# A decoder layer in fp32 on one core: the value products of five cross attention units in one pass over four shared PSUM banks, and weight turns alternating with query projections

## The reference, cut to what matters

```
q = (queries @ Wq + bq).reshape(b_s, nq, H, D_K).transpose(0, 2, 1, 3)
k = (keys @ Wk + bk).reshape(b_s, nk, H, D_K).transpose(0, 2, 1, 3)
v = (values @ Wv + bv).reshape(b_s, nk, H, D_V).transpose(0, 2, 1, 3)
att = jnp.einsum('bhqd,bhkd->bhqk', q, k) / jnp.sqrt(jnp.float32(D_K))
att = att * attention_weights
att = jnp.where(attention_mask, -jnp.inf, att)
att = jax.nn.softmax(att, axis=-1)
out = jnp.einsum('bhqk,bhkd->bhqd', att, v)
out = out.transpose(0, 2, 1, 3).reshape(b_s, nq, H * D_V)
return out @ Wo + bo
```

## Time and profile before

| | |
|---|---|
| median of 3 runs | 582.8 us (581.6 to 583.47) |
| the profiled execution | 583.38 us, span 581.5 us, mean granted TensorE clock 0.995 |
| PE busy | 562.7 us, 97% of the span |
| DVE busy | 441.7 us, 76% |
| ACT busy | 326.0 us, 56% |
| POOL busy | 232.7 us, 40% |
| stages 2 to 6 (161.12 to 337.88 us) | 176.76 us, of which PE is busy 175.99 |

### The profile page before, as it was taken

The page is one execution under the profiler, slowest core; times in us unless marked ns, Lnnn a source line. Parts: engine busy times, 40 slices in busy tenths (PEclk is TensorE's granted clock), DMA queues, the critical chain, the costliest instruction groups (busy, mean ns, idle before and its releaser), DMA issues.

```text
span 581.5 us, 11126 instructions
## 1 busy us (share of the span) xinstructions
PE 562.7 (97%) x3656; PEld 426.0 (73%) x3656; DVE 441.7 (76%) x838; ACT 326.0 (56%) x1005; POOL 232.7 (40%) x228
## 2 busy tenths in 40 slices
PE   8999999999999999999999999999999999999992
PEld 6547566788697978888788787878777776676661
DVE  3999999999886879958788679866677556566651
ACT  3632424368869796795976939715232245555220
POOL 1010110307590834477334581626235433444434
PEclk9999999999999999999999999999999999999997
DMA  8920004162741231522316107892654443343424
GB/s 302 349 100 2 1 1 174 45 217 91 275 152 68 93 127 34 185 74 90 130 37 218 55 23 231 261 393 94 172 129 83 64 67 62 54 67 48 60 31 45
DMA packets 36183, 68.37 MB, mean 118 GB/s; under 512 B 5504, under 2 KB 29024, under 8 KB 33632
## 3 DMA queue, kind: packets, MB, share of 16 engines
q1 hardware_dynamic: 28208, 57.99, 29.9%
q0 software_dynamic: 6784, 8.95, 9.3%
q10 hardware_dynamic: 1136, 0.73, 0.4%
HBM read 56.62 MB, written 15.25 MB: 124 GB/s over the span
## 4 chain that ended last, share of the span: by engine, by line
PE 56%; DVE 20%; DMA 9%; issue 8%; POOL 4%; ACT 2%; POOLq 0%; DVEq 0%; SPq 0%
PE pb L744 7%; DMA out_dram<-R 6%; PE pb L636 6%; DVE R L1140 6%; PE pb L499 6%; PE pb L601 6%; PE pb L549 6%; PE pb L565 5%; PE pb L516 4%; PE pb L648 4%; PE pb L778 4%; DVE R L1163 3%; PE pb L613 2%; PE pb L569 2%; DMA out_dram<-R,hidx 2%
## 5 line engine op out<-in xcount | busy, mean ns | idle before, releaser
L896 ACT ACTIVATE R<-R,mx 128x154 f32<-128x154 f32 x256 | 104.4, 415 | 0.1
L1761 POOL DMA_INDIRECT out_dram<-R x36 | 56.1, 1557 | 82.9 <-DMA out_dram<-R 41.7
L744 PE MATMUL pb<-R 128*128 x256 | 81.0, 459 | 0.0
L1022 ACT ACTIVATE R<-R 128x352 f32<-128x352 f32 x36 | 17.9, 497 | 90.4 <-DVE R L1572 74.9
L744 PEld LDWEIGHTS pb<-R 128*128 128x128 f32 x256 | 46.2, 190 | 20.4
L499 PE MATMUL pb<-xnT,wq 128*128 128x256 f32 x256 | 58.2, 383 | 0.0
L887 ACT ACTIVATE R<-pb,bq 128x256 f32<-128x256 f32 x64 | 30.1, 474 | 47.9 <-PE pb L499 47.8
L499 PEld LDWEIGHTS pb<-xnT,wq 128*128 128x128 f32 x256 | 47.7, 190 | 7.8 <-issue 1.2
L908 ACT COPY R<-pb 128x512 f32<-128x512 f32 x80 | 40.8, 614 | 18.4 <-PE pb L549 18.3
L1685 POOL DMA_INDIRECT xs_dram<-xn,pos x32 | 31.7, 991 | 47.3 <-DVE pos L1324 39.0
L896 ACT ACTIVATION_READ_ACCUMULATOR R<-R,mx 128x1 f32 x256 | 49.5, 193 | 0.0
(11 more groups left out here) (202 smaller groups left out, 1179.1 us busy)
## 6 DMA issues: line engine op xcount, KB each, us to landing
R<-in_fside_dram SPq DMA_DIRECT2D x16, 1232.0 KB, 5.6
R<-in_L_ffn_w_dram SPq DMA_DIRECT2D x16, 352.0 KB
R<-in_mask_dram SPq DMA_DIRECT2D x16, 308.0 KB, 2.9
R<-xs_dram SPq DMA_DIRECT2D x32, 129.0 KB, 2.1
KV<-in_ebias_dram SPq DMA_DIRECT2D x2, 1440.0 KB
out_dram<-x SPq DMA_DIRECT2D x4, 512.0 KB
R<-in_L_ffn_w_dram SPq DMA_DIRECT2D x8, 256.0 KB, 4.3
x<-in_x_dram SPq DMA_DIRECT2D x3, 512.0 KB, 10.9
```

The source lines that it names most:

```text
L744: ins = e.matmul(pb[:, u.i, 0:F], xsT[:, s % 2, k, :], ew13[:, bass.ds(w_reg[s] * 1408 + q * 704 + k * F, F)], start=(k == 0), stop=(k == 1))
L896: ins = e.activation(att[t % 3][:, h, :], att[t % 3][:, h, :], ACT.Exp, bias=mx[:, a4, 1, h:h + 1], accum_out=mx[:, a4, 2, h:h + 1])
L1761: e.indirect_dma_start(out=out, out_offset=bass.IndirectOffsetOnAxis(ap=to.bitcast(U32), axis=0), in_=rows, in_offset=None, compute_op=ALU ...
```

## The change

It touches units 1 to 5 (`WHOLE`), that is, stages 2 to 6.

1. **One product a unit.** `product_whole` takes four banks once. Half 0 of the heads goes to columns 0 to 255, half 1 to columns 256 to 511. All 16 matmuls of 128 rows come first, then all 16 of 32 rows. DVE drains it with two additions of 2 banks x 512 columns each instead of four of 2 banks x 256.
2. **Turns and queries alternate.** PE does 4 queries, then 2 banks of turned weights and 1 query in turn, four times, then the last 2 banks. ACT copies in the same order.
3. **What stood between moves.** `place` goes ahead of the product, `turned(*BETWEEN[n])` behind it. On ACT `normalise` and `turned` come one after the other behind the last of the ten weight copies. On DVE the product comes behind the last `top`.
4. `combined` reads `oT` in the order 0, 1, 4, 5, 2, 3, 6, 7, so that its first four steps need only the first addition.

The core of the diff:

```
+            def product_whole(u8):
+                b = u8 // 4
+                uses = [u for g in range(2) for u in bank.take_pair(("av", u8, g))]
...
+                for hf in range(2):
+                    cols = slice(256 * hf, 256 * hf + 256)
+                    for n in range(8):
+                        u, to = uses[n // 2], 64 * (n % 2 ^ n // 4)
+                        w.wait_ge(free[u.e], u.empty)
+                        e.matmul(pb[to:to + 64, u.i, cols], vm[b][:, 8 * hf + n, :], turned_in(hf, n),
+                                 start=(hf == 0), stop=False)
+                for hf in range(2):
+                    cols = slice(256 * hf, 256 * hf + 256)
+                    for g in range(2):
+                        for r in (0, 2, 1, 3):
+                            u, to = uses[2 * g + r // 2], 64 * (r % 2 ^ g)
+                            ins = e.matmul(pb[to:to + 64, u.i, cols], vr[b][32 * r:32 * r + 32, 2 * hf + g, :],
+                                           turned_in(hf, 8 + g)[32 * r:32 * r + 32, :], start=False, stop=(hf == 1))
+                            if hf and r % 2:
+                                ins.then_inc(full[u.i], 1)
+            def turned_amid_queries(u8):
...
+                queries(u8 + 2, range(0, 4))
+                for n in range(5):
+                    for hf, k in divmod(2 * n, 5), divmod(2 * n + 1, 5):
+                        weights_turned(u8, hf, k)
+                    if n < 4:
+                        queries(u8 + 2, range(4 + n, 5 + n))
-                    for j in range(8):
-                        d = bank["av", u8, j // 4, j // 2 % 2, 0]
+                    for j in (0, 1, 4, 5, 2, 3, 6, 7):
+                        d = bank["av", u8, j // 2 % 2, 0] if u8 in WHOLE else bank["av", u8, j // 4, j // 2 % 2, 0]
                 elif u8 < 7:
-                    queries(u8 + 1)
+                    turned_amid_queries(u8 - 1)
+                    if u8 in (4, 6):
+                        place(u8 // 2 - 2)
+                    product_whole(u8 - 1)
+                    if u8 in BETWEEN:
+                        turned(*BETWEEN[u8])
```

On ACT:

```
+                elif u8 < 7:
+                    queries(u8 + 1, range(0, 4))
+                    for n in range(5):
+                        for hf, k in divmod(2 * n, 5), divmod(2 * n + 1, 5):
+                            evacuate(u8 - 1, hf, k, k + 1)
+                        if n < 4:
+                            queries(u8 + 1, range(4 + n, 5 + n))
+                    if u8 in BETWEEN:
+                        normalise(*BETWEEN[u8])
+                        turned(*BETWEEN[u8])
+                    else:
+                        exps(t0, range(0, 2))
```

On DVE:

```
+            def product_whole(u8):
...
+                for g in range(2):
+                    u, v = bank["av", u8, g, 0], bank["av", u8, g, 1]
...
+                    e.tensor_tensor(
+                        oT[:, :, :].rearrange("p (f b) q -> p f b q", f=2)[:, :, 2 * g:2 * g + 2, :],
...
+                            [P, 2, 2, 256]), ALU.add).then_inc(free[u.i], 1)
-                if u8 < 7:
-                    product(u8 - 1, 0)
+                if u8 == 1:
+                    product(0, 0)
                 if u8 in (4, 6):
                     place(u8 // 2 - 2)
                 if u8 < 7:
                     top(t1, (0, H))
-                product(u8 - 1, 1)
+                if u8 - 1 in WHOLE:
+                    product_whole(u8 - 1)
+                else:
+                    product(u8 - 1, 1)
```

More of the change, by code:

```diff
@@ L138 @@
 PHI = [("k", 0), ("k", 1), ("q", 0), ("q", 1)]
+WHOLE = range(1, 6)
 SPLIT = [(1, 0), (3, 3)]
@@ L572, in product, with turned_in @@
                             ins.then_inc(full[u.i], 1)
+            def product_whole(u8):
+                b = u8 // 4
+                uses = [u for g in range(2) for u in bank.take_pair(("av", u8, g))]
+                def turned_in(hf, n):
+                    d = bank["pT", u8, hf, n // 2]
+                    w.wait_ge(free[d.i], d.drained)
+                    return pT[:, hf, n, :]
+                for hf in range(2):
[15 more added lines that the diff above has]
+            def turned_amid_queries(u8):
+                for n in range(3):
+                    d = bank["con", B - 1, n]
+                    w.wait_ge(free[d.i], d.drained)
+                queries(u8 + 2, range(0, 4))
[4 more added lines that the diff above has]
+                        queries(u8 + 2, range(4 + n, 5 + n))
             def values(u8, between, amid=None, turning=None):
@@ L691, in _ @@
                     queries(2, range(7))
+                    values(0, None, None, lambda: queries(2, range(7, 8)))
                 elif u8 < 7:
-                    queries(u8 + 1)
+                    turned_amid_queries(u8 - 1)
[4 more added lines that the diff above has]
+                        turned(*BETWEEN[u8])
                 else:
                     shared_out(*FILL[6])
-                values(u8 - 1, BETWEEN.get(u8), (lambda: place(u8 // 2 - 2)) if u8 in (4, 6) else None,
-                       (lambda: queries(2, range(7, 8))) if u8 == 1 else None)
+                    values(6, BETWEEN[7])
                 if u8 - 1 in FILL and u8 < 7:
@@ L902, in evacuate @@
                 for i in range(4 if u8 else 0):
-                    d = bank["av", u8 - 1, hf, i // 2, i % 2]
+                    d = bank["av", u8 - 1, i // 2, i % 2] if u8 - 1 in WHOLE else bank["av", u8 - 1, hf, i // 2, i % 2]
                     w.wait_ge(full[d.i], d.filled)
@@ L972, in _ @@
                 gating = u8 >= 3 and u8 % 2
-                if u8 < 7:
-                    queries(u8 + 1, range(7 if u8 == 1 else 8))
-                evacuate(u8 - 1, 0, 0, 5)
                 if u8 == 1:
+                    queries(2, range(7))
+                    evacuate(0, 0, 0, 5)
                     queries(2, range(7, 8))
[L978 to L981, removed]
+                    evacuate(0, 1, 0, 3)
                     exps(t0, range(0, 2))
-                evacuate(u8 - 1, 1, 3, 5)
-                if u8 in BETWEEN:
-                    turned(*BETWEEN[u8])
+                    evacuate(0, 1, 3, 5)
+                elif u8 < 7:
[11 more added lines that the diff above has]
+                else:
+                    evacuate(6, 0, 0, 5)
+                    evacuate(6, 1, 0, 3)
+                    normalise(*BETWEEN[7])
+                    evacuate(6, 1, 3, 5)
+                    turned(*BETWEEN[7])
                 if u8 == 7:
@@ L1252, in product @@
                                     ALU.add).then_inc(free[u.i], 1)
+            def product_whole(u8):
+                w.wait_ge(in_bv, 16)
+                d = bank["wo", u8 - 1, 1]
+                w.wait_ge(full[d.i], d.filled)
+                for g in range(2):
+                    u, v = bank["av", u8, g, 0], bank["av", u8, g, 1]
+                    w.wait_ge(full[u.i], u.filled)
+                    w.wait_ge(full[v.i], v.filled)
+                    e.tensor_tensor(
+                        oT[:, :, :].rearrange("p (f b) q -> p f b q", f=2)[:, :, 2 * g:2 * g + 2, :],
+                        pb[:, u.i:u.i + 2, :].rearrange("p b (f q) -> p f b q", f=2),
+                        bvT[:, :].rearrange("p (f b a) -> p f b a", f=2, a=1)[:, :, 2 * g:2 * g + 2, :].broadcast_to(
+                            [P, 2, 2, 256]), ALU.add).then_inc(free[u.i], 1)
             def attended(u8, qs=(0, 1)):
```

## The result

| | before | after | ratio |
|---|---|---|---|
| median of the runs, us | 582.4 (581.6 to 583.5) | 588.65 (585.4 to 591.7) | 1.0108, interval 1.0061 to 1.0155 |
| profiled execution, us | 583.38 | 587.99 | |
| its span, us | 581.5 | 586.2 | |
| its mean granted clock | 0.995 | 0.993 | |

The change makes the kernel 1.1% slower. The forecast of 586.8 us had the sign and the mechanism, and is 1.9 us short; the range, up to 590.0, held the time. The four runs after lie 6 us apart where those before lie within 2.

A forecast was written before the change was run, and what follows sets the result against it. PE was taken to set the pace, with ACT and DVE about 5 us slack a stage. Delays less savings gave +4.0 on the profiled 583.4, so 587.4; less 0.6, a median of 586.8 us, range 582.5 to 590.0.

The forecast's parts named there:

- The whole product: PE, one product a unit: 4.80 us instead of 5.28, saving 0.48 a unit, 2.4 over five.
- The alternation and the earlier turns: PE alternating turns and queries costs nothing; POOL's scaling is ready in time by 0.3 us, costed at 0.
- Combined in stage 2: PE starts `combined` at 183.1 instead of 182.94, behind DVE's first addition: +0.2 us, stage 2's saving gone.
- The late copies: ACT's copies to `xnT` wait for PE; the first exponential comes 2.05 us later in each of stages 2 to 5.
- Stage 2 into 3: DVE's sums wait for late exponentials; PE is 1.5 us late at stage 3's third query, 0.2 already counted.
- Stage 3 into 4: Chain from the `xnT` copies has no slack: stage 4's scores let PE go at 231.65 instead of 228.15, +3.5 us.
- Stage 4: PE saves 0.48 us; DVE's slack of 3.1 covers the 2.55 asked, so PE leaves at +3.0.
- Stage 5 into 6: DVE had waited only 0.53 us before stage 6's scores, so these and PE start 4.5 us late.
- rival 1: Late copies stay in ACT's slack and the saved shape changes count: 580.4 us; chance 0.15.
- Rival 2: Stage 2's delay does not reach PE's third query, so about half the loss: 585.4 us; chance 0.13.
- rival 3: Stage 4's slack on DVE is used up too, PE leaves it at +5.5: 589.3 us; chance 0.09.
- rival 4: Matmuls in a row still pay 0.96 us of shape changes, stages 4 to 6 lose 1.4: 588.2 us; chance 0.04.

The follow-up runs named there:

- second profile: The change itself, unaltered, profiled and timed once more: 590.2 us, ratio 1.0125.
- late-turned run: Kernel before, with only `turned` moved behind the second half's product in stages 2 to 5: 589.2 us, ratio 1.0113.
- the last one: Change with `turned` ahead of the product in stages 3 and 5, behind it in 2 and 4 with eight exponentials ahead of the copies: 580.4 us.
- the run without alternation: Change with five exponentials ahead of the `xnT` copies, and all eight queries before the ten turns on PE and ACT: 581.5 us, ratio 0.9980.
- the filled versions: Change with five or eight exponentials of tile t0 on ACT ahead of the `xnT` copies in stages 2 to 5: 581.1 us (five), 580.8 us (eight).
- the fill in stage 2: Change with five exponentials ahead of the `xnT` copies in stage 2 only: 588.3 us, ratio 1.0108.
- the version with the fill in stages 3 to 5: Change with five exponentials ahead of the `xnT` copies in stages 3 to 5, not in stage 2: 583.0 us, ratio 1.0016.
- idle products: Change with eight unused 64-column products on PE within the first tile's scores of stages 4 and 6: 587.9 us, ratio 1.0091.

## Why the prediction was right, and what it lacked

The forecast was a sum stage by stage, and the second profile of the change measures it without a fall of the clock in these stages:

| from the scores of stage 2 to | forecast | first profile | second profile |
|---|---|---|---|
| stage 3 | +0.2 | +0.20 | +0.20 |
| stage 4, second tile | +3.5 | +3.65 | +3.66 |
| stage 5 | +3.0 | +3.05 | +3.06 |
| stage 6, second tile | +4.5 | +4.49 | +4.51 |
| stage 7 | +4.0 | +5.61, 3.94 without the clock | +3.96 |

- **The whole product.** Forecast 4.80 us. In the timeline of PE after, from the last weight turn (176.40) to the first record of `turned` (181.26), less the turn's own 0.11, it is 4.75; read in the same way, each half of before took 2.59 (175.85 to 178.55), so 0.43 is saved where 0.48 was forecast. The chain above has 4.65, by modelled ends. Over five stages the gain is 2.6 us by the late-turned run and 2.37 by the last one, for 2.4. By the Trainium skill (TensorE: Matmul & The Clock Gate, "The cost: per-tile semaphore tail"), 26.3 ns for each signal left out, an estimate would be 2.9. Neither run reaches that, and they differ by too much to tell half of it.
- **The alternation and the earlier turns** cost nothing: the run without alternation is level, and PE has no wait for POOL's scaling in stages 2 to 6, before or after.
- **Combined in stage 2** waits 0.48 for DVE and starts 0.23 later than before, counted from the scores of stage 2; +0.2 was forecast, +0.20 found at stage 3.
- **The late copies.** ACT waits 2.64 us for `turned` in stage 2, and 10.9 over the four stages. The first exponential, at 183.2 by the forecast, is at 183.02, with the 0.3 us between the traces 183.3.
- **Stage 2 into 3.** DVE's reciprocal waits 1.81 (forecast about 2), PE's third query 1.10 where the forecast had over 1.
- **Stage 3 into 4** was right in size, and the wait in another place: not at the second tile's scores (0.56, which before has as well), but 1.53 in the middle of the first tile's. The third pair of banks is the one that `combined` used, and DVE frees it behind the router. Before had no wait there.
- **Stage 4.** DVE had slack of 3.1 against 2.55 asked; 0.6 should be left, and the wait that answers to the 0.72 of the earlier trace rows is now

```profile
267.39 2.85 DVE L1263 TENSOR_TENSOR R<-pb,R 128x924 f32<-128x924 f32 x3 [0.63 <-PE pb L517]
```

- **Stage 5 into 6.** No wait is left on DVE, where the earlier trace rows had 0.53. PE waits 1.28 and 0.56 us in the scores of stage 6, for about 2 forecast.
- **Rivals.** The slack of rival 1 did not exist. What it forecast is nearly what the filled versions measure, 580.8 to 581.1 for its 580.4, once ACT's order gives it that slack. Its price was off by its own terms: the paragraph on DVE gives up the saving of stage 2 and adds 0.2, so 1.7 us are left of the 2.4, which is 581.1. Rival 2 fell with +3.65 at stage 4, where it has +1.6, rival 3 with +3.06 at stage 5, where it has +5.5, rival 4 with a product of 4.75, where it needs 5.28.
- **A slip.** One query to the next is 0.87 us in the earlier trace rows, not 0.864. Over the ten slots of a half that is 0.02 us, and no step hangs on it.

The step that came out short is the last: "583.4 + 4.0 = 587.4", and the same on the medians. It took the path's delay for the whole delay and the clock for given. For the profiled execution it nearly holds, 587.99. The medians are 6.2 and 7.7 us over before. By the profiles 3.9 to 4.0 of that is the path, and by full-clock times 3.7 to 4.1 (a scale that gives the clock too much). The rest, 2 to 4 us, goes with lower mean clocks. The two profiles of the change have one fall each ahead of the end of the span. The four runs at 0.985 to 0.988 would have about three or four (an estimate: the clock lost, less 2.5 us for the end, by 1.7 us each). None of these has a trace, so where their falls stand is open.

That PE's new waits bring them is likely and not shown. For it: the version with five exponentials ahead has no such waits in stages 4 and 6, and clocks of 0.991 to 0.996 in twelve runs, as before has. Against it: of the seven places in four profiles where PE waits 1.28 to 1.54 us and 0.56 us more in stage 4 or 6 (two profiles of the change, the fill in stage 2, the late turned inputs alone) the clock fell at two; and the version with the fill in stages 3 to 5, whose profile has no wait over 1.1 us in these stages, has runs at 0.989 and 0.990 too, and the kernel before has one at 0.990.

So the path was forecast, and that the range held the median was in part luck: what carried it from 586.8 to 588.65 was the clock, no term of the sum and not rival 3. The second set of runs has its median at 590.2, just outside the 590.0.

## What to carry to other kernels

An instruction put later on the engine that bounds costs nothing there; ask which in-order queue waits for it, and what stands behind the wait in that queue. Here 1 us of turned inputs held back 32 exponentials in each of four stages, and moving five of them ahead of the wait won back everything. And where an edit opens waits of 1 to 2 us in an engine that was gapless, look at the mean clock and the spread of the runs too. Here 22 runs of the kernel before, timed together, lie within 3.0 us and the ten of the change within 6.2, and the medians rose by 2 to 4 us more than the path explains.

## What the runs showed of the hardware

TensorE's granted clock fell from 2.4 to 1.2 GHz for 3.4 us behind short waits: behind 1.28 + 0.56 us with 0.80 us of work between them (after, 308.2 us), 1.54 + 0.56 (fill in stage 2, 232.5 us) and 0.47 + 0.56 (idle products, 232.1 us). Up to these waits the engine had been busy and at full clock for over 10 us.

The same waits in other executions did nothing. The wait in the linear attention at about 30 us shows it best, since every profile has it: it was 1.33 to 1.42 us in six of the twelve, and no fall came behind it, and 1.47 to 2.01 us in the other six, where a fall came behind 1.47, 1.51 and 1.75 and none behind 1.50, 1.65 and 2.01.

A fall in stage 4 or 6 made the way from the second tile's scores to the next stage 1.52 to 1.67 us longer (36.18 and 36.23 us for 34.66, 35.35 for 33.68), which is the price to be reckoned for one.

At the end of every profile, with PE at rest, the clock fell too and stayed at half for the last 5 to 8 us of the span. That lowers the mean clock, and PE has nothing left to lose by it.
